# A vision-transformer block on one core: the second norm in two tile groups, expert gates by tanh, the router behind two half blocks

## The chip, the core and the metric

The kernel runs on one core of one Trainium2 chip. Its time is the device time of one execution in microseconds; before the change three executions took 165.94, 166.53 and 167.59 us (median 166.53 us). The profile is of one further execution. TensorE is called PE below, its weight loads PEld, VectorE DVE, ScalarE ACT, GpSimd POOL and SyncE SP.

## The reference

Sixteen images of 3x96x96 are cut into 36 patches each, with four shifted copies beside each channel; patches are normalised, multiplied by a 3840x192 matrix, and a class token is put in front, which gives 16 x 37 = 592 tokens of 192 numbers. One transformer layer follows:

```python
h = h + attention(layernorm(h))          # 12 heads of 16, bias by distance
h = h + ffn(layernorm(h))                # the second norm is this one

def ffn(x):                              # per token
    probs = softmax(x @ router_w)        # 8 experts
    gates, idx = top_k(probs, 2)
    gates = gates / sum(gates)
    g, u = silu(x @ w_gate[e]), x @ w_up[e]
    routed = sum of gates[e] * ((g * u) @ w_down[e])
    shared = (silu(x @ ws_gate) * (x @ ws_up)) @ ws_down     # 768 wide
    alpha = sigmoid(x @ sg_w + sg_b)
    return alpha * shared + (1 - alpha) * routed
```

Everything is float32. All eight experts are computed densely for all tokens; the gates of the ones that were not chosen are zero.

## The kernel before

**Tiles.** The 592 tokens lie in five tiles of 128 (`TILES`; the last has 80 real tokens) when tokens are on the partitions, and in two halves of 296 columns (`HALF`) when features are. Each large product is split into float16 high and low parts: a value X is kept as `XAh` (high, features 0 to 127), `XAl` (its low part), `XB` (high, features 128 to 191, twice) and `YC` (low of these). So one 128x296 product takes five matmuls, k = 0 to 4. k = 0 and 1 read `XAh`, k = 2 `XB`, k = 3 `XAl`, k = 4 `YC`.

**Stages.** Patches and tokens (to about 33 us), first norm (to 44 us), attention (to 80 us), second norm (80 to 88 us), feed-forward (from 85.85 us to the end).

**Second norm.** `wo(t)` on PE writes the attention output of tile t into PSUM, `add_attention` on DVE adds the residual, then follow statistics (`residual`, L1039), `variances` (L1049), a square root on ACT (`root`, L731), five small DVE steps (`rsqrt`, L999) and `normed` (L1060), all with one pass over five tiles for the small steps. `NORMS` (L64) lists the groups of tiles of each pass: the first norm has a group of three and a group of two, the second norm one of five. ACT duplicates 64 columns of each tile (`copies`), PE transposes (two per tile), ACT writes high parts (`high_parts`), DVE low parts (`low_parts`), each once for tiles 0 to 2 (part 0) and once for tiles 3 and 4 (part 1). `keep_warm` is a run of matmuls whose results are not used.

**Feed-forward.** There are 18 blocks f of 128 hidden columns (6 shared, 12 of experts) and two halves, so 36 half blocks i. `gu(i)` is ten matmuls (gate m = 0 and up m = 1), `silu_step(i)` on ACT, `product(i)` on DVE, `act_high(i)` on ACT and `act_low(i)` on POOL follow, and `down(f)` is fifteen matmuls for the five tiles. `gu(i)` waits for `product(i - 2)`, whose PSUM banks it takes. The PE order is gu(0) with the router in its middle, gu(1), gu(2), gu(3), then per block two `gu` and one `down` two blocks behind. A matmul needs half 0 only from tiles 0 to 2 (columns 0 to 295 of 0 to 383).

**Router and gates.** `router` (L558) is thirty matmuls of nine columns. DVE copies the logits out (L1205) and picks the two largest in chains of small dependent steps (`choose_first`, `second_largest`, `choose_second`, `gate_sum`, `gate_split`), which stand between products 0 to 4. ACT takes exponentials of logits. The gates are transposed on PE (`gates`), copied by ACT (`gate_copy`), written to DRAM and broadcast from there, to be used from block 6 on. Between its silu steps ACT also rounds the next weights (`ffn_high`), and DVE makes their low parts (`ffn_low`). The order on each engine is written out by hand; each engine runs its list in order and waits on semaphores.

Of the kernel before, what the change touches and what calls it, by code (L numbers as in the profile page):

```python
# [58 lines left out]
GATE_STEP = 6  # L59
ABUF = 3  # L60
# [3 lines left out]
NORMS = ((0, range(0, 5), 5), (10, range(0, 3), 10), (10, range(3, 5), 15), (20, range(0, 5), 20))  # L64
# [18 lines left out]
def vit_kernel(nc, x_inner, x_ring, w_inner, w_ring, gb, consts, j_rev, ind, tok_b, cls, tab,  # L83
               aw_a, aw_b, aw_c, f_a, f_b, f_d, gate_rows, out):
    with ExitStack() as ctx:
# [92 lines left out]
        def split(p):  # L178
# [28 lines left out]
                   a_first a_xh a_xsq a_s0 a_ring a_bw a_sqr a_cs a_aw a_wh a_sqrt a_hi a_k a_q a_vh a_exp a_pth a_chi a_e a_dup a_sig a_gt  # L207
                   a_fw a_silu a_ah
                   v_one v_ind v_pad v_aw0 v_jm v_jr v_xl v_fold v_wl v_awl v_mk v_stat v_h v_hn v_lo  v_vm v_xr v_sg v_max v_sub
                   v_rows v_cn v_rd v_lg v_gate v_gx v_fw v_hf v_acc v_fin v_al v_bn  # L210
# [14 lines left out]
        def wparts(c0, c1):  # L225

            return [WAh[:, c0:c1], WAl[:, c0:c1], WB[:, c0:c1], WAh[:, c0:c1], WC[:, c0:c1]]

# [66 lines left out]
        def _(pe):  # L295
# [207 lines left out]
            def wo(t):  # L503

                need = min(2 * (t + 1), PAIRS)
                pe.wait_ge(S["a_chi"], need)
                tok = slice(t * P, (t + 1) * P)
                o = PS[:, (3, 3, 4, 4, 5)[t], D * (t % 2):D * (t % 2) + D]
                mm(o, CA[:, tok], awst[:, 0, OC:OC + D], start=(t % 2 == 0), stop=False, skip_group_check=True)
                last = mm(o, CC[:, tok], awst[0:CROWS, 2, OC:OC + D], start=False, stop=True, skip_group_check=True)  # L510
                last.then_inc(S["p_wo"], 1)
# [60 lines left out]
            def gu(i):  # L572

                f, half = divmod(i, 2)
# [8 lines left out]
                for m in range(2):  # L583
                    if i == 0 and m == 1:
                        router()
                    w5 = (Ah[:, m, fc], Al[:, m, fc], Bw[:, m, fc], Ah[:, m, fc], Bw[:, m, fc])
                    for k, (w, x) in enumerate(zip(w5, yparts(cols))):
                        if i < 2 and m == 0:
                            tokens_ready(1, i, k)
                        last = mm(PS[:, 3 + 2 * (i % 2) + m, 0:HALF], w, x, start=(k == 0), stop=(k == 4))  # L590
# [44 lines left out]
        def _(act):  # L635
# [196 lines left out]
            def act_high(i):  # L832
                f, half = divmod(i, 2)
# [9 lines left out]

            for i in range(2 * FT + 1):
                if 0 <= i - 1 - GATE_STEP < 2:
                    gate_copy(i - 1 - GATE_STEP)
                if i < 2 * FT:
# [10 lines left out]
        def _(pool):  # L858
# [20 lines left out]
            def act_low(i):  # L879
                f, half = divmod(i, 2)  # L880
# [15 lines left out]
        def _(dve):  # L896
# [271 lines left out]
            def add_attention(t):  # L1168
                dve.wait_ge(S["p_wo"], (2, 2, 4, 4, 5)[t])
                return V.scalar_tensor_tensor(  # L1170
                    out=h2[:, t, :], in0=PS[:, (3, 3, 4, 4, 5)[t], D * (t % 2):D * (t % 2) + D],
# [24 lines left out]
            def over8(v):  # L1196
                return v.unsqueeze(2).to_broadcast([P, TILES, 8])

            m1, s1, m2, s2, den, rd_ = (small[:, i, :] for i in (32, 33, 34, 35, 36, 37))
# [4 lines left out]
            dve.wait_ge(S["p_r"], 1)  # L1204
            V.tensor_scalar(lg[:, :, :], PS[:, 7, 0:9 * TILES].rearrange("p (t e) -> p t e", t=TILES), 1.0 / XW, None,  # L1205
                            ALU.mult).then_inc(S["v_lg"], 1)
            dve.wait_ge(S["v_lg"], 1)
            V.tensor_reduce(m1, l8, AX.X, ALU.max).then_inc(S["v_bn"], 1)
            dve.wait_ge(S["v_bn"], bn[0] + 1)
            gstep(V.tensor_tensor(g8[:, 0], l8, over8(m1), ALU.subtract))  # L1210

            def choose_first():
                gstep(V.tensor_tensor(g8[:, 2], l8, over8(m1), ALU.is_equal))
# [4 lines left out]
            def second_largest():  # L1218
                gstep(V.scalar_tensor_tensor(out=g8[:, 5], in0=g8[:, 4], scalar=-3e38, in1=l8, op0=ALU.mult,
                                             op1=ALU.add))  # L1220
                gstep(V.tensor_reduce(m2, g8[:, 5], AX.X, ALU.max))
                gstep(V.tensor_tensor(g8[:, 6], g8[:, 5], over8(m2), ALU.is_equal))

            def choose_second():
# [3 lines left out]
                gstep(V.tensor_tensor(g8[:, 9], g8[:, 8], g8[:, 4], ALU.add))  # L1228

            def gate_sum():  # L1230
# [183 lines left out]
```

## Time and profile before

| what | value |
|---|---|
| median of three executions | 166.53 us |
| profiled execution, device time | 166.45 us |
| its span, first to last instruction | 164.6 us |
| outside the span | 1.85 us |
| PE busy | 147.1 us |
| DVE busy | 116.2 us |
| ACT busy | 89.7 us |
| POOL busy | 42.0 us |
| mean granted clock | 0.986 |

All times inside a trace count from the first instruction of the span. A timeline row gives the start, the duration, the engine, the source line, the operation and, in brackets, how long the engine was idle before it and what ended that. A row with x5 merges five instructions of one kind.

### The profile page before, as it was taken

The page shows a single profiled execution, that of the slowest core. Times are in us where ns is not written, and L with a number is a line of the kernel's source. Part 1 is how long each engine was busy: PE and PEld are TensorE (multiplying, and loading weights), DVE is VectorE, ACT ScalarE, POOL GpSimd, SP SyncE. Part 2 cuts the span into 40 slices and gives each one's busy share as a digit, 9 for nine tenths or more (in the row PEclk, how much of TensorE's full clock was granted, in tenths as well). Part 3 has the DMA queues.
Part 4 walks back from the last instruction along what each step waited for, and adds up shares of the span by engine and source line. Part 5 has one row for each costly group of instructions (what it writes and reads, how often), then busy time and mean ns, then how long its engine had stood idle before and what let it go on. Part 6 is the DMA issues. An engine that isn't in the chain of part 4 may idle for free.

```text
span 164.6 us, 4269 instructions
## 1 busy us (share of the span) xinstructions
PE 147.1 (89%) x1717; PEld 113.5 (69%) x1717; DVE 116.2 (71%) x285; ACT 89.7 (54%) x198; POOL 42.0 (26%) x55
## 2 busy tenths in 40 slices
PE   0449999999989998979998999999899999999992
PEld 0217778863658997868645677888668788788781
DVE  6299969799897678957673797785885832732753
ACT  0498797561679335453457697655465343334440
POOL 0000001000000000000000345368576677487330
PEclk9999999999999999999997899999999999999998
DMA  5999974900000000002995000258000000000003
GB/s 142 387 361 381 300 190 100 415 19 0 0 0 4 4 4 4 4 0 67 378 405 210 0 0 0 63 207 329 2 4 0 0 4 2 2 4 0 0 0 111
DMA packets 7391, 16.89 MB, mean 103 GB/s; under 512 B 800, under 2 KB 3612, under 8 KB 7372
## 3 DMA queue, kind: packets, MB, share of 16 engines
q1 hardware_dynamic: 7012, 16.29, 28.5%
q10 hardware_dynamic: 360, 0.34, 0.7%
q8 instruction: 13, 0.21, 0.6%
q14 instruction: 6, 0.05, 0.1%
HBM read 16.15 MB, written 0.47 MB: 101 GB/s over the span
## 4 chain that ended last, share of the span: by engine, by line
PE 57%; DVE 24%; ACT 7%; issue 6%; ACTq 3%; POOL 2%; DVEq 0%; POOLq 0%
PE PS L590 19%; PE PS L618 11%; PE PS L436 4%; PE PS L323 3%; PE PS L344 2%; PE PS L346 2%; PE PS L410 2%; PE PS L347 2%; DVE mx L1123 2%; DVE xsq L1127 2%; DVE hn L1064 2%; PE PS L455 2%; DVE vhl L1268 2%; PE PS L310 2%; POOL vhl L876 1%
## 5 line engine op out<-in xcount | busy, mean ns | idle before, releaser
L885 POOL TENSOR_TENSOR kq<-vhl,kq 128x296 f16<-128x296 f32 x35 | 29.4, 841 | 87.0 <-ACT kq L837 86.8
L1268 DVE SCALAR_TENSOR_TENSOR vhl<-PS,vhl 128x296 f32<-128x296 f32 x36 | 16.8, 466 | 21.9 <-POOL vhl L876 12.1
L830 ACT ACTIVATE vhl<-PS 128x296 f32<-128x296 f32 x36 | 15.0, 416 | 26.5 <-PE PS L590 26.4
L837 ACT ACTIVATE kq<-vhl 128x296 f16<-128x296 f32 x36 | 16.0, 445 | 5.4 <-DVE vhl L1268 5.4
L876 POOL TENSOR_TENSOR vhl<-vhl,xs 128x296 f32<-128x296 f32 x14 | 12.6, 900 | 5.6 <-issue 4.8
L1257 DVE TENSOR_TENSOR vhl<-vhl,xs 64x296 f32<-64x296 f32 (+1 forms) x18 | 10.2, 565 | 2.8 <-ACT vhl L830 2.6
L590 PE MATMUL PS<-XAh,piece 128*128 128x296 f16 x48 | 10.8, 310 | 0.3
L590 PE MATMUL PS<-XAh,slab 128*128 128x296 f16 x48 | 10.0, 291 | 0.9 <-DVE vhl L1268 0.9
L344 PE MATMUL PS<-whl,xhl 128*128 128x193 f16 (+1 forms) x40 | 10.6, 266 | 0.0
L346 PE MATMUL PS<-whl,xhl 128*128 128x193 f16 (+1 forms) x40 | 10.6, 265 | 0.0
L347 PE MATMUL PS<-whl,xhl 128*128 128x192 f16 (+1 forms) x40 | 10.5, 262 | 0.0
L373 PE MATMUL PS<-WAh 128*128 128x512 f16 x44 | 10.3, 380 | 0.1
L936 DVE SCALAR_TENSOR_TENSOR we<-slab,gbs,we 128x192 f32<-128x192 f32 x24 | 8.2, 414 | 3.1 <-ACT we L674 3.1
L310 PE MATMUL PS<-slab,gbs 128*32 128x192 f32 x60 | 4.5, 396 | 6.6 <-DMA slab<-in_w_inner_dram 6.6
L590 PE MATMUL PS<-XAh,xsq 128*128 128x296 f16 x48 | 10.0, 290 | 0.0
L618 PE MATMUL PS<-slab,kq 128*128 128x192 f16 x90 | 8.4, 246 | 0.3 <-DVE t L1291 0.3
L618 PE MATMUL PS<-piece,kq 128*128 128x192 f16 x90 | 8.4, 246 | 0.0
L618 PE MATMUL PS<-xsq,kq 128*128 128x192 f16 x90 | 8.2, 246 | 0.1
L618 PEld LDWEIGHTS PS<-slab,kq 128*128 128x128 f16 x90 | 7.5, 98 | 0.8 <-issue 0.6
L618 PEld LDWEIGHTS PS<-xsq,kq 128*128 128x128 f16 x90 | 7.5, 98 | 0.5 <-issue 0.3
L323 PE MATMUL PS<-xsq,one 128*32 128x296 f32 (+1 forms) x32 | 5.7, 484 | 2.4 <-ACT xsq L642 2.4
L618 PEld LDWEIGHTS PS<-piece,kq 128*128 128x128 f16 x90 | 7.6, 98 | 0.3
(215 smaller groups left out, 395.3 us busy)
## 6 DMA issues: line engine op xcount, KB each, us to landing
slab<-in_w_inner_dram SPq DMA_DIRECT2D x3, 960.0 KB, 9.5
xs<-gate_rows_dram SPq DMA_DIRECT2D x8, 296.0 KB, 5.9
xs<-in_x_inner_dram SPq DMA_DIRECT2D x3, 592.0 KB, 10.6
stage<-in_f_a_dram SPq DMA_DIRECT2D x2, 768.0 KB, 4.8
stage<-in_f_b_dram SPq DMA_DIRECT2D x2, 768.0 KB, 6.4
stage<-in_f_d_dram SPq DMA_DIRECT2D x2, 576.0 KB, 7.9
xhl<-in_f_a_dram SPq DMA_DIRECT2D x1, 768.0 KB, 8.8
xhl<-in_f_b_dram SPq DMA_DIRECT2D x1, 768.0 KB, 10.3
```

Source lines behind the costliest of these rows:

```text
L323: last = mm(PS[q:q + 32, 6 + half, 0:HALF], one[0:K, :].to_broadcast([K, 32]), xsqv[0:K, j, half * HALF:(half + 1) * HALF], start=(j < 4), ...
L344: mm(o, xh[0:K, j, tok], wh[0:K, j, :], start=(j == 0 and t % 2 == 0), stop=False, skip_group_check=True)
L346: mm(o, xl[0:K, j, tok], wh[0:K, j, :], start=False, stop=False, skip_group_check=True)
L347: last = mm(o[:, 0:D], xh[0:K, j, tok], wl[0:K, j, :], start=False, stop=(j == CHUNKS - 1), skip_group_check=True)
L373: mm(PS[:, bank, :], WAh[:, 0:P], WAh[:, 0:512], start=True, stop=True)
L590: last = mm(PS[:, 3 + 2 * (i % 2) + m, 0:HALF], w, x, start=(k == 0), stop=(k == 4))
L618: last = mm(o, a[:, f % ABUF, tok], w[:, f % PT_, :], start=(f in (0, ST) and t % 2 == 0 and k == 0), stop=(f in (ST - 1, FT - 1) and k == ...
L830: A(silu[:, i % 2, :], PS[:, 3 + 2 * (i % 2), 0:HALF], ACT.Silu, scale=1.0 / XW).then_inc(S["a_silu"], 1)
L837: A(ah[:, f % ABUF, half * HALF:(half + 1) * HALF], hf[:, i % 3, :], ACT.Copy).then_inc(S["a_ah"], 1)
L876: G.tensor_tensor(sgate[:, i % 2, :], silu[:, i % 2, :], Gb[:, f_expert(f)[0], cols], ALU.mult).then_inc(S["g_sg"], 1)
L885: G.tensor_tensor(al[:, f % ABUF, cols], hf[:, i % 3, :], ah[:, f % ABUF, cols], ALU.subtract).then_inc(S["g_al"], 1)
L1268: V.scalar_tensor_tensor(out=hf[:, i % 3, :], in0=PS[:, 4 + 2 * (i % 2), 0:HALF], scalar=SH / XW, in1=src[:, i % 2, :], op0=ALU.mult, op1= ...
```

## The change

- `NORMS`: the second norm runs in a group of tiles 0 to 2 and one of tiles 3 and 4. Tile 2's attention output moves to bank 4 alone, those of 3 and 4 to bank 5.
- DVE: variances of the first group stand before the residual of tile 3; tile 4's residual and the second group's variance stand behind the first group's `normed`; its `rsqrt` and `normed` behind the low parts of the first group; then product 0, and only then the low parts of the second group.
- The first four half blocks are now (f, half) = (0,0), (1,0), (0,1), (1,1). PE does gu(0) and gu(1), then the transposes of tiles 3 and 4, four `keep_warm` matmuls, the whole router, then gu(2). In block 0 the order of the ten matmuls is k = 0 and 1 for both m, and then k by k.
- `down(0)` and `down(1)` wait for four half blocks, where down(0) waited for two.
- ACT: a square root for the second group, a one-element silu ahead of `silu_step(0)`, then the copies and high parts of the second group. Three exponentials go; two tanh (five values per partition each) come behind `act_high(1)` and `act_high(3)`.
- Gates: with d the difference of the two largest logits, the first gate is (1 + tanh(d/2))/2 and the second (1 - tanh(d/2))/2, and alpha = (1 + tanh(l/2))/2. The chain on DVE is `choose_first` (with the copy of the logits) behind product 1, the second choice behind product 2, `gate_split` behind product 3, `gate_values` behind product 4.
- `keep_warm` in the second norm: 5 and 3 matmuls where it was 6, 4, 4 and 3.

```diff
-NORMS = ((0, range(0, 5), 5), (10, range(0, 3), 10), (10, range(3, 5), 15), (20, range(0, 5), 20))
+NORMS = ((0, range(0, 5), 5), (10, range(0, 3), 10), (10, range(3, 5), 15), (20, range(0, 3), 20),
+         (20, range(3, 5), 25))
+def half_block(i):
+    return ((0, 0), (1, 0), (0, 1), (1, 1))[i] if i < 4 else divmod(i, 2)
...
-            keep_warm(6, 6)
-            for name, count, n in (("v_h", 3 * TILES, 4), ("v_stat", 20, 4), ("v_stat", 21, 3)):
-                pe.wait_ge(S[name], count)
-                keep_warm(6, n)
-            transposes(1, (0, 1, 2), range(TILES))
+            keep_warm(6, 5)
+            pe.wait_ge(S["v_stat"], 22)
+            keep_warm(6, 3)
+            transposes(1, (0, 1, 2), range(3))
...
+                    if f == 1 and half == 0:
+                        transposes(1, (0, 1, 2), (3, 4))
+                        keep_warm(7, 4)
+                        router()
...
-                pe.wait_ge(S["a_ah"], 2 * f + 2)
-                pe.wait_ge(S["g_al"], min(2 * f + 2, 2 * FT - 1))
+                pe.wait_ge(S["a_ah"], max(2 * f + 2, 4))
+                pe.wait_ge(S["g_al"], min(max(2 * f + 2, 4), 2 * FT - 1))
...
-            copies(1, range(TILES))
+            copies(1, range(3))
             high_parts(1, (0, 1, 2), 0)
-            high_parts(1, (0, 1, 2), 1)
-            act.wait_ge(S["v_lg"], 1)
-            A(small[:, 30, :], lg[:, :, 8], ACT.Exp, scale=-1.0).then_inc(S["a_sig"], 1)
-            A(small[:, 31, :], lg[:, :, 8], ACT.Exp).then_inc(S["a_sig"], 1)
-            act.wait_ge(S["v_gate"], 1)
-            A(g8[:, 1], g8[:, 0], ACT.Exp).then_inc(S["a_e"], 1)
+            root(4)
+            A(small[:, 46, 0:1], one[:, :], ACT.Silu)
...
+            silu_step(0)
+            copies(1, (3, 4))
+            high_parts(1, (0, 1, 2), 1)
...
+                if i == 2:
+                    alpha_tanh()
+                if i == 4:
+                    gate_tanh()
...
-            residual(1, add_attention, (2, 3))
-            residual(1, add_attention, (4,))
+            residual(1, add_attention, (2,))
             variances(3)
+            residual(1, add_attention, (3,))
             rsqrt(3)
             dve.wait_ge(S["p_t"], TILES)
-            normed(1, range(TILES))
+            normed(1, range(3))
+            residual(1, add_attention, (4,))
+            variances(4)
             low_parts(1, (0, 1, 2), 0)
-            low_parts(1, (0, 1, 2), 1)
+            rsqrt(4)
+            normed(1, (3, 4))
...
-            for i in range(2 * FT):
+            product(0)
+            low_parts(1, (0, 1, 2), 1)
+            for i in range(1, 2 * FT):
                 product(i)
-                if i == 0:
+                if i == 1:
                     choose_first()
-                if i == 1:
+                if i == 2:
                     second_largest()
-                if i == 2:
                     choose_second()
                 if i == 3:
-                    gate_sum()
+                    gate_split()
                 if i == 4:
-                    gate_split()
+                    gate_values()
```

## Rows read from the trace of the kernel before

**Rows 1.** The page: busy time by engine, and PE's granted clock in 40 slices.

```profile
PE 147.1 (89%) x1717; PEld 113.5 (69%) x1717; DVE 116.2 (71%) x285; ACT 89.7 (54%) x198; POOL 42.0 (26%) x55
PEclk9999999999999999999997899999999999999998
```

**Rows 2.** Windows: length, busy time (instructions) per engine, granted clock, DMA share, GB/s.

```profile
83.93:88.30 4.37, 3.62 (x45) 2.28 (x46) 2.78 (x8) 3.85 (x10) 0.00 (x0) 0.99 1.03 408
88.30:91.79 3.49, 3.49 (x22) 2.09 (x18) 1.12 (x5) 2.25 (x5) 0.00 (x0) 0.52 0.08 31
91.80:98.67 6.87, 6.67 (x57) 4.91 (x56) 6.25 (x24) 6.14 (x14) 3.19 (x5) 1.00 0.00 0
```

**Rows 3.** Timeline of PE, from the last attention output into the feed-forward.

```profile
79.53 0.49 PE L510 MATMUL PS<-awst,we 97*128 97x192 f32 x2
...
85.85 0.41 PE L590 MATMUL PS<-XAh,piece 128*128 128x296 f16 x2
...
87.56 0.17 PE L566 MATMUL PS<-WAh,XAh 128*128 128x9 f16 x1 [0.45 <-DVE wring L1074]
...
91.81 0.42 PE L590 MATMUL PS<-XAh,piece 128*128 128x296 f16 x2
...
98.67 0.41 PE L590 MATMUL PS<-XAh,piece 128*128 128x296 f16 x2
```

**Rows 4.** Timeline of ACT, second norm and the first half blocks.

```profile
83.91 1.42 ACT L753 ACTIVATE hn<-hn 128x64 f32<-128x64 f32 x5 [1.78 <-DVE hn L1064]
85.23 0.47 ACT L746 ACTIVATE XAh<-PS 128x384 f16<-128x384 f32 x1
...
85.97 0.39 ACT L746 ACTIVATE XAh<-PS 128x256 f16<-128x256 f32 x1
...
86.65 1.28 ACT L821 ACT_TABLE_LOAD   x1
...
89.46 1.28 ACT L830 ACT_TABLE_LOAD   x1
90.75 0.42 ACT L830 ACTIVATE vhl<-PS 128x296 f32<-128x296 f32 x1
...
93.27 0.42 ACT L830 ACTIVATE vhl<-PS 128x296 f32<-128x296 f32 x1 [0.50 <-PE PS L590]
...
93.92 0.83 ACT L729 ACTIVATE slab<-stage 128x768 f16<-128x768 f32 x1
...
96.45 0.44 ACT L837 ACTIVATE kq<-vhl 128x296 f16<-128x296 f32 x1
```

**Rows 5.** Timeline of DVE in the second norm.

```profile
80.47 0.34 DVE L1170 SCALAR_TENSOR_TENSOR h<-PS,h 128x192 f32<-128x192 f32 x1
80.84 0.36 DVE L1046 BATCH_NORM_STATS2 bst<-h 128x6 f32<-128x192 f32 x1
...
82.61 0.19 DVE L1005 RECIPROCAL small<-small 128x5 f32<-128x5 f32 x1 [0.71 <-ACT small L735]
...
83.50 1.54 DVE L1064 TENSOR_SCALAR hn<-h,mv,small 128x192 f32<-128x192 f32 x5
```

**Rows 6.** The chain that ended last: start, length, line; one `down`, two `gu`.

```profile
102.25 1.24 PE PS L618 x15
103.49 2.52 PE PS L590 x20
```

**Rows 7.** Timeline of DVE, last low part, product 0 and gate steps.

```profile
87.01 0.41 DVE L1074 SCALAR_TENSOR_TENSOR wring<-PS,XB 64x256 f16<-64x256 f32 x1
88.50 0.21 DVE L1205 TENSOR_SCALAR whl<-PS 128x45 f32<-128x45 f32 x1 [1.09 <-PE PS L568]
...
91.27 0.47 DVE L1268 SCALAR_TENSOR_TENSOR vhl<-PS,vhl 128x296 f32<-128x296 f32 x1 [2.10 <-ACT vhl L830]
...
92.96 0.68 DVE L1219 SCALAR_TENSOR_TENSOR whl<-whl 128x40 f32<-128x40 f32 x1
```

**Rows 8.** Timeline of POOL: the low part of product 0.

```profile
92.85 0.74 POOL L885 TENSOR_TENSOR kq<-vhl,kq 128x296 f16<-128x296 f32 x1 [67.48 <-ACT kq L837]
```

More of the change, by code:

```diff
@@ L59 @@
 GATE_STEP = 6
+STEADY = [(k, m) for m in range(2) for k in range(5)]
+FIRST = [(0, 0), (1, 0), (0, 1), (1, 1)] + [(k, m) for k in range(2, 5) for m in range(2)]
 ABUF = 3
@@ L507, in wo @@
                 tok = slice(t * P, (t + 1) * P)
-                o = PS[:, (3, 3, 4, 4, 5)[t], D * (t % 2):D * (t % 2) + D]
-                mm(o, CA[:, tok], awst[:, 0, OC:OC + D], start=(t % 2 == 0), stop=False, skip_group_check=True)
-                last = mm(o, CC[:, tok], awst[0:CROWS, 2, OC:OC + D], start=False, stop=True, skip_group_check=True)
+                mm(attention_out(t), CA[:, tok], awst[:, 0, OC:OC + D], start=(t in (0, 2, 3)), stop=False,
+                   skip_group_check=True)
+                last = mm(attention_out(t), CC[:, tok], awst[0:CROWS, 2, OC:OC + D], start=False, stop=True,
+                          skip_group_check=True)
                 last.then_inc(S["p_wo"], 1)
@@ L572, in gu @@
             def gu(i):
-                f, half = divmod(i, 2)
+                f, half = half_block(i)
                 if i % (2 * PT_) == 0:
@@ L582, in gu @@
                 fc = slice(f % PT_ * P, (f % PT_ + 1) * P)
[L583 to L590, printed above, removed]
+                w5 = [(Ah[:, m, fc], Al[:, m, fc], Bw[:, m, fc], Ah[:, m, fc], Bw[:, m, fc]) for m in range(2)]
+                x5 = yparts(cols)
+                for k, m in FIRST if f == 0 else STEADY:
+                    if f == 0 and m == 0:
+                        tokens_ready(1, half, k)
+                    last = mm(PS[:, 3 + 2 * (i % 2) + m, 0:HALF], w5[m][k], x5[k], start=(k == 0), stop=(k == 4))
                 last.then_inc(S["p_gu"], 1)
@@ L832, in act_high @@
             def act_high(i):
-                f, half = divmod(i, 2)
+                f, half = half_block(i)
                 act.wait_ge(S["v_hf"], i + 1)
@@ L879, in act_low @@
             def act_low(i):
-                f, half = divmod(i, 2)
+                f, half = half_block(i)
                 cols = slice(half * HALF, (half + 1) * HALF)
@@ L1197, in over8 @@
                 return v.unsqueeze(2).to_broadcast([P, TILES, 8])
-            m1, s1, m2, s2, den, rd_ = (small[:, i, :] for i in (32, 33, 34, 35, 36, 37))
+            m1, s1, m2, s2, dif, both = (small[:, i, :] for i in (32, 33, 34, 35, 36, 37))
             l8 = lg[:, :, 0:8]
             rank = cst_rank[:, :].unsqueeze(1).to_broadcast([P, TILES, 8])
[L1204 to L1210, printed above, removed]
-            def choose_first():
+            def choose_first():
+                dve.wait_ge(S["p_r"], 1)
+                V.tensor_scalar(lg[:, :, :], PS[:, 7, 0:9 * TILES].rearrange("p (t e) -> p t e", t=TILES), 1.0 / XW,
+                                None, ALU.mult).then_inc(S["v_lg"], 1)
+                dve.wait_ge(S["v_lg"], 1)
+                gstep(V.tensor_reduce(m1, l8, AX.X, ALU.max))
                 gstep(V.tensor_tensor(g8[:, 2], l8, over8(m1), ALU.is_equal))
@@ L1227, in choose_second, with gate_values @@
                 gstep(V.tensor_tensor(g8[:, 8], rank, over8(s2), ALU.is_equal))
-                gstep(V.tensor_tensor(g8[:, 9], g8[:, 8], g8[:, 4], ALU.add))
-            def gate_sum():
-                dve.wait_ge(S["a_e"], 1)
-                gstep(V.tensor_tensor(g8[:, 10], g8[:, 9], g8[:, 1], ALU.mult))
-                gstep(V.tensor_reduce(den, g8[:, 10], AX.X, ALU.add))
-                gstep(V.reciprocal(rd_, den))
-            def gate_split():
-                dve.wait_ge(S["a_sig"], 2)
-                gstep(V.tensor_scalar(small[:, 40:42, :], small[:, 30:32, :], 1.0, None, ALU.add))
-                gstep(V.reciprocal(small[:, 42:44, :], small[:, 40:42, :]))
-                gstep(V.tensor_scalar(small[:, 38, :], small[:, 42, :], 1.0 / (SH * SW), None, ALU.mult))
-                gstep(V.scalar_tensor_tensor(out=small[:, 39, :], in0=rd_, scalar=1.0, in1=small[:, 43, :],
-                                             op0=ALU.mult, op1=ALU.mult))
-                V.tensor_tensor(Gf[:, :, :], g8[:, 10], over8(small[:, 39, :]), ALU.mult).then_inc(S["v_gx"], 1)
+            def gate_split():
+                dve.wait_ge(S["a_sig"], 1)
+                V.tensor_scalar(small[:, 38, :], small[:, 31, :], 0.5 / (SH * SW), 0.5 / (SH * SW), ALU.mult,
+                                ALU.add).then_inc(S["v_gate"], 1)
+                gate[0] += 1
+                gstep(V.tensor_scalar(both, small[:, 31, :], -0.25, 0.25, ALU.mult, ALU.add))
+            def gate_values():
+                dve.wait_ge(S["a_sig"], 2)
+                gstep(V.tensor_tensor(small[:, 40, :], small[:, 30, :], both, ALU.mult))
+                V.tensor_tensor(small[:, 42, :], both, small[:, 40, :], ALU.add).then_inc(S["v_gate"], 1)
+                gate[0] += 1
+                gstep(V.tensor_tensor(small[:, 43, :], both, small[:, 40, :], ALU.subtract))
+                V.tensor_tensor(g8[:, 9], g8[:, 4], over8(small[:, 42, :]), ALU.mult).then_inc(S["v_gate"], 1)
+                gate[0] += 1
+                gstep(V.tensor_tensor(g8[:, 10], g8[:, 8], over8(small[:, 43, :]), ALU.mult))
+                V.tensor_tensor(Gf[:, :, :], g8[:, 9], g8[:, 10], ALU.add).then_inc(S["v_gx"], 1)
             def product(i):
```

20 lines of the change are left out of this document (15 added, 5 removed).

## The prediction

> **What bounds the kernel now.** I read the page first: PE is busy 89% of the span, with its clock below full speed in two neighbouring slices only [rows 1]. So PE's own list sets the time wherever it does not wait. In the steady part of the feed-forward two half blocks take 2.52 us and one down product 1.24 us, with nothing between them [rows 6]; the change touches neither number. What it can win is where PE waits or runs slowly, and the windows by stage show where that is [rows 2]: from 83.93 to 88.30 PE is busy 3.62 of 4.37 us, much of it transposes, and from 88.30 to 91.79 it is nominally full but at a granted clock of 0.52.
>
> PE's timeline gives the marks [rows 3]: the last attention product ends at 79.53 + 0.49 = 80.02, gu(0) starts at 85.85, the router at 87.56, gu(2) at 91.81, gu(6), right behind down(0), at 98.67. The useful work between gu(0) and gu(6) is six half blocks (3 x 2.52), the router (87.56 to 88.30, 0.74) and a down product (1.24): 9.54 us [rows 3, 6]. It takes 98.67 - 85.85 = 12.82 us.
>
> The reasons are in ACT's timeline [rows 4]: a table load of 1.28 us for the exponentials and a second one at 89.46 for silu, so that the first silu starts at 90.75 although gu(0) was done about 89.5 (five of the fifteen matmuls that fill the 3.49 us from 88.30 [rows 2]). Product 0 runs at 91.27 for 0.47 [rows 7] and releases gu(2) at 91.81. PE's slow clock was hidden by that: gu(1) ended just as product 0 did. Since gu(2) starts when both are there, a full clock alone would have won next to nothing.
>
> **The norm in two groups.** The limit becomes the last attention product, because tile 3 shares a bank with tile 4: residual of tile 3 at 80.02 + 0.04 = 80.06, 0.34 for it, 0.36 for its statistics with 0.03 between [rows 5], so 80.8 (the 0.04 is my estimate of a hand-over). The three-tile variance and the root lie beside the wait for PE (tile 2's product is two products earlier, an estimated 1.5 us, since the last part of one alone takes 0.49 [rows 3]) and cost nothing; that cover is gone only if they take longer than this wait. From the reciprocal to normed is 83.50 - 82.61 = 0.89 [rows 5]: normed at 81.7 instead of 83.50. Normed to the first high part took 85.23 - 83.50 = 1.73 [rows 4, 5]; with three copies of 1.42/5 = 0.28 ahead of it instead of five it is no longer than that. High part to gu(0): 85.85 - 85.23 = 0.62 [rows 3, 4]. So gu(0) starts at 81.7 + 1.73 + 0.62 = 84.05, **1.8 us earlier**. Tile 4's residual, statistics and variance (0.34 + 0.36 and some 0.5 for the rest) stand on DVE between normed (ends 82.7) and the low parts, which wait for the high part until 83.9 in any case: about hidden, 0.1 us at worst, and PE has gu(0)'s first four or six matmuls meanwhile.
>
> **Block 1 ahead of the router.** gu(0) and gu(1) take 2.52 and end at 86.6. Behind ACT's two high parts (start 83.45, about 0.85) come the root (0.2), a table load of 1.28 and the one-element silu (0.2), so silu 0 starts at 86.0 and ends at 86.4. Queued behind it are the two copies (0.56). DVE has meanwhile done the low parts (to 85.0), rsqrt (0.89) and normed of two tiles (0.6), to 86.5; product 0 takes it to 86.95, beside PE's transposes. The transposes of two tiles end at 87.2. From the first high part of the small group to the end of its last low part is 87.01 + 0.41 - 85.97 = 1.45 [rows 4, 7]: 88.65. The router goes to 89.4, and gu(2) starts there, 2.4 us earlier than at 91.81. PE idles about 0.75 us before the router; the four warming matmuls lie in that wait.
>
> **Gates.** Copy of the logits and five steps of 0.21 [rows 7], with some 0.02 between them: 1.4 us from 89.6 to 91.0, just before product 2. silu(2) starts when gu(2) ends (90.65), at 90.8. On ACT silu(2) to act_high(3) was 96.45 - 93.27 = 3.18 to its start [rows 4], with a rounding of 0.83 twice in it; the tanh adds 0.2: act_high(3) at 94.2 at the earliest, 0.44 long. On DVE product 2 ends at 91.7; the eight steps of the second choice now all stand behind it, seven of them one after another, 1.6 us if all take 0.21, 2.0 us if the one beside POOL takes 0.68 again [rows 7]: 93.3 to 93.7, so product 3 ends at 93.8 to 94.15. gu(5) waits for it from 93.2: a **new wait on PE of 0.6 to 1.0 us**, where before the two chains stood behind different products. I take 1.0. gu(5) ends at 95.5. down(0) now waits for POOL's low part 3: act_high(3) ends at 94.65, POOL's 0.74 [rows 8] takes it to 95.5. Both end together. down(0) to 96.8: gu(6) starts at 96.8 instead of 98.67. gate_split and gate_values are eight steps where gate_sum and gate_split were eight; the last one ends near 96.4, before gu(6) ends at 98.05 and the transposes of the gates want it. Nothing.
>
> **From there on** every dependence is the same, so the gain is carried to the end: all weights were loaded by 88.5 (the DMA share falls to 0.08 after 88.30 [rows 2]), and the broadcast of the gates starts as much earlier as its first use. No DMA issue is moved.
>
> **The sum.** 98.67 - 96.8 = 1.9 us. Against the profiled execution, 166.45 us with 164.6 us of span and 1.85 us around it, that is 164.6 us. The median of the runs shown, 166.53, is 0.08 above it, which I neglect.
>
> **Two rules of the pages.** A load at 86.65 ends at 87.93 and the one at 89.46 is followed by silu at 90.75, within 0.01 us of its end: a switch costs 1.28 us here [rows 4]. The Trainium skill, page "ScalarE: Activation LUTs", section "What ACT_TABLE_LOAD costs", adds a drain of about 1.38 us to each, 2.66 us in all; by that, silu 0 would start about 1.4 us later than I have it and the gain would shrink to about 0.5 us. The rows speak against it.
>
> Whether tanh needs a load of its own beside silu no row shows. The same page, section "Table sets: the hidden batching unit", lists tanh in the sets of exp and of sigmoid and names no set that has silu. By that rule each tanh would bring two loads; that is the third rival.
>
> **Rivals.** (1) *The slow clock moves onto the path.* PE was granted 0.52 for 3.49 us after a stretch with transposes, waits and nine-column matmuls [rows 2]. The new order has more dense work in it (block 1, the warming matmuls), but also a wait and the router ahead of gu(2). If the low stretch covers gu(2) and gu(3), ten matmuls take 1.26/0.52 = 2.4 us; silu 2 and all behind it move by 1.15, while gu(3)'s delay is absorbed by the wait before gu(5). Gain 1.9 - 1.15 = 0.75: 165.7 us.
>
> (2) *DVE and ACT become the bound.* Before gu(6) DVE was busy 6.25 and ACT 6.14 of 6.87 us [rows 2]. They now get gu(2) to gu(5) with the same lists in a shorter time. If POOL's writes slow more of the small steps as at 92.96 (0.68 for 0.21) [rows 7], say two more, the second choice ends 1 us later and PE waits that long. Gain 0.9: 165.5 us.
>
> (3) *Slower: tanh reloads tables.* A load of 1.28 ahead of each tanh and one ahead of the silu that follows it. Silu 3 and with it product 3 move by 2.56, less the 0.4 to 0.8 us in which product 3 waits for DVE anyway; act_high(3) and down(0) move by 2.56; the second pair pushes silu 5, the later silu steps and gate_copy by 2.56 again, of which ACT's idle time there (about 1 us before silu 6) takes 1.0. In sum about 2.56 + 2.56 - 1.0 = 4.1 us: 164.6 + 4.1 = 168.7 us. It decides as soon as ACT loses more than 1.9 us in this stretch.
>
> (4) *The head start is lost before the router.* If silu 0, with the copies behind it, comes later than I have it, the transposes, the small group's parts and the router go with it one for one. It would have to be 2.4 us late to lose all of gu(2)'s head start: 166 to 166.5 us.
>
> **Chances.** My forecast (gain 1.4 to 2.5) 0.52, rival 1 0.18, rival 2 0.13, rival 3 0.06, rival 4 or something not seen 0.11, of which half slower. A measurement here can tell about 1% from no change, 1.67 us, so faster means under 164.86. The forecast's centre is only 0.26 us under that line: I give it two thirds of its 0.52 for faster, and 0.07 for a larger gain or a slower reference elsewhere, 0.42. Slower than 168.2: rival 3 and half of the unseen, 0.12. Same: 0.46. The range goes from a gain of 3.1 us (the stalls before gu(5) and down(0) gone too) to 166.7, which holds rivals 1, 2 and most of 4: 163.4 to 166.7; outside are rival 3 and the unseen on both sides.
>
> **What would show it.** One table load fewer (sqrt, silu; none at a tanh). Normed of three tiles at 81.6 to 81.8, gu(0) at 83.9 to 84.1, gu(2) at 89.3 to 89.6, gu(6) at 96.6 to 97.0, and from gu(6) to the end the same 65.9 us as before. A wait of PE before gu(5) released by a DVE product, and none before gu(2) released by one. The granted clock from 85 to 92 tells rival 1. I am wrong if normed does not start before 82.5, if an ACT table load stands next to a tanh, or if PE waits over 1.5 us before gu(5) or down(0).

## The result and the profile after

The changed kernel took 164.48 us (median of 4, 163.98 to 165.09) against 166.24 us before (median of 4); the ratio is 0.9887, 95% interval 0.9846 to 0.9929. The forecast was 164.6 us, range 163.4 to 166.7. Five further rounds later gave 164.41 us and 0.9882 (0.9853 to 0.9910). Medians in this document are over all executions of a kernel, ratios leave out those over 1.5% above its fastest. So the number was right, in part by luck. The share that the prediction gave to each cause was not, as the experiments below show.

The profiled execution took 164.49 us, with a span of 162.7 us. The page's opening lines answer to [rows 1]:

```profile
span 162.7 us, 4264 instructions
PE 143.3 (88%) x1712; PEld 111.7 (69%) x1712; DVE 117.3 (72%) x290; ACT 88.4 (54%) x198; POOL 42.2 (26%) x55
PEclk9999999999999999999999999999999999999999
```

The clock stays up in this trace. PE's timeline, with the rows that answer to [rows 3] (start, duration, engine, line, operation, idle time before it):

```profile
78.91 0.49 PE L523 MATMUL PS<-awst,we 97*128 97x192 f32 x2
...
83.33 0.66 PE L601 MATMUL PS<-XAh,piece 128*128 128x296 f16 x4 [0.67 <-ACT XAh L761]
...
88.11 0.17 PE L579 MATMUL PS<-WAh,XAh 128*128 128x9 f16 x1 [0.76 <-DVE wring L1100]
...
88.86 0.66 PE L601 MATMUL PS<-XAh,piece 128*128 128x296 f16 x4
...
93.98 0.42 PE L601 MATMUL PS<-XAh,piece 128*128 128x296 f16 x2 [1.19 <-DVE vhl L1297]
...
95.34 1.40 PE L629 MATMUL PS<-piece,kq 128*128 128x192 f16 x15
...
96.57 0.41 PE L601 MATMUL PS<-XAh,piece 128*128 128x296 f16 x2
```

These are the last attention product (end 79.40), gu(0), the router, gu(2), gu(5), down(0) and gu(6). The first mark stands 0.62 us earlier than before's 80.02. The difference is there 52 us ahead of it, in the patch stage, which the change does not touch (these rows are from the traces of before and of the changed kernel; at 14 us the two still agree within 0.2 us):

```profile
27.79 0.52 PE L310 MATMUL PS<-wring,gbs 96*32 96x192 f32 x4
27.18 0.52 PE L323 MATMUL PS<-wring,gbs 96*32 96x192 f32 x4
```

Two traces of the changed kernel differ there by as much (27.18 and 27.70), and over all traces of this study the first mark lies between 79.10 and 80.47. Marks behind it must therefore be compared as distances from it, and this is done from here on. **gu(6) starts 17.17 us after the last attention product, where it was 18.65: 1.48 us won.** From gu(6) to the end of the span it is 66.13 us, where it was 65.93. So within the trace the change wins 1.3 us, and 0.6 us of the shorter span lies in the early part. The runs say 1.8 and 2.2 us. The rest of that is not explained: the first mark is at 80.06 on average in the four traces with the old norm and order (before and tanh alone, twice each) and at 79.62 in the ten others, but the first group lies wholly within the range of the second, so whether the change also shortens the early part is not shown.

Windows by stage, to be held against [rows 2] (length, busy time and instructions of PE, PEld, DVE, ACT, POOL, then granted clock, DMA share, GB/s):

```profile
79.40:88.11 8.71, 7.10 (x44) 3.87 (x42) 6.93 (x28) 5.36 (x16) 0.21 (x1) 1.00 1.00 387
88.11:96.57 8.46, 7.27 (x85) 5.66 (x86) 6.82 (x27) 5.67 (x14) 3.07 (x5) 1.00 0.03 9
```

In both stages PE now idles more than a microsecond. ACT's timeline shows the tables, as [rows 4] did:

```profile
83.68 1.28 ACT L835 ACT_TABLE_LOAD   x1
84.97 0.20 ACT L835 ACTIVATE small<-one 128x1 f32<-128x1 f32 x1
85.08 0.40 ACT L849 ACTIVATE vhl<-PS 128x296 f32<-128x296 f32 x1
...
90.31 0.42 ACT L849 ACTIVATE vhl<-PS 128x296 f32<-128x296 f32 x1 [2.49 <-PE PS L601]
90.63 0.44 ACT L856 ACTIVATE kq<-vhl 128x296 f16<-128x296 f32 x1
90.97 0.20 ACT L839 ACTIVATE small<-whl 128x5 f32<-128x5 f32 x1
91.07 0.83 ACT L744 ACTIVATE slab<-stage 128x768 f16<-128x768 f32 x1
```

One load, for silu, then silu 0 at once; the tanh at 90.97 stands between its neighbours with no load, and ACT waits 2.49 us for PE ahead of silu 2. On DVE (normed of three tiles, the second choice, product 3) and POOL (low part 3), the rows that answer to [rows 5, 7, 8]:

```profile
81.03 0.96 DVE L1090 TENSOR_SCALAR hn<-h,mv,small 128x192 f32<-128x192 f32 x3
...
91.22 0.73 DVE L1245 SCALAR_TENSOR_TENSOR whl<-whl 128x40 f32<-128x40 f32 x1
91.98 0.20 DVE L1247 TENSOR_REDUCE small<-whl 128x5 f32<-128x40 f32 x1
...
92.98 0.44 DVE L1254 TENSOR_TENSOR whl<-cst,small 128x40 f32<-128x40 f32 x1
93.46 0.47 DVE L1297 SCALAR_TENSOR_TENSOR vhl<-PS,vhl 128x296 f32<-128x296 f32 x1
```

```profile
92.62 0.74 POOL L911 TENSOR_TENSOR kq<-vhl,kq 128x296 f16<-128x296 f32 x1 [0.73 <-ACT kq L856]
94.48 0.75 POOL L911 TENSOR_TENSOR kq<-vhl,kq 128x296 f16<-128x296 f32 x1 [1.12 <-ACT kq L856]
```

### The profile page after: what moved, and what is told of

Its sections match the earlier page's. It is cut to its first block, busy times and chain, and to the rows that moved or that the text cites. A ratio compares the mean times of both kernels' runs of the same rounds, so it can differ in the third digit from the quotient of the medians.

```text
span 162.7 us, 4264 instructions
## 1 busy us (share of the span) xinstructions
PE 143.3 (88%) x1712; PEld 111.7 (69%) x1712; DVE 117.3 (72%) x290; ACT 88.4 (54%) x198; POOL 42.2 (26%) x55
## 4 chain that ended last, share of the span: by engine, by line
PE 62%; DVE 20%; ACT 6%; issue 5%; ACTq 3%; POOL 2%; DVEq 0%; POOLq 0%
PE PS L601 22%; PE PS L629 11%; PE PS L449 4%; PE PS L336 3%; PE PS L423 2%; PE PS L359 2%; PE PS L357 2%; PE PS L360 2%; DVE mx L1149 2%; DVE xsq L1153 2%; PE PS L468 2%; PE PS L323 2%; POOL vhl L902 1%; PE PS L498 1%; DVE vhl L1297 1%
## 5 line engine op out<-in xcount | busy, mean ns | idle before, releaser
L1297 DVE SCALAR_TENSOR_TENSOR vhl<-PS,vhl 128x296 f32<-128x296 f32 x36 | 16.8, 465 | 20.3 <-POOL vhl L902 12.1
L601 PE MATMUL PS<-XAh,piece 128*128 128x296 f16 x48 | 9.6, 289 | 1.9 <-DVE vhl L1297 1.2
L357 PE MATMUL PS<-whl,xhl 128*128 128x193 f16 (+1 forms) x40 | 10.3, 257 | 0.0
L359 PE MATMUL PS<-whl,xhl 128*128 128x193 f16 (+1 forms) x40 | 10.3, 257 | 0.0
L386 PE MATMUL PS<-WAh 128*128 128x512 f16 x39 | 9.6, 380 | 0.3 <-DVE small L1033 0.2
```

What stands on the lines that cost most here:

```text
L357: mm(o, xh[0:K, j, tok], wh[0:K, j, :], start=(j == 0 and t % 2 == 0), stop=False, skip_group_check=True)
L359: mm(o, xl[0:K, j, tok], wh[0:K, j, :], start=False, stop=False, skip_group_check=True)
L601: last = mm(PS[:, 3 + 2 * (i % 2) + m, 0:HALF], w5[m][k], x5[k], start=(k == 0), stop=(k == 4))
L1297: V.scalar_tensor_tensor(out=hf[:, i % 3, :], in0=PS[:, 4 + 2 * (i % 2), 0:HALF], scalar=SH / XW, in1=src[:, i % 2, :], op0=ALU.mult, op1= ...
```

## The experiments

Each was timed beside the kernel before on its chip; ratios are to that kernel. The medians of before were 166.15, 166.35 and 166.58 us on the three chips of the experiments, so medians of two rows can differ by 0.2 to 0.4 us through the chip alone; where that matters, go by the ratios. "To gu(6)" is the distance from the end of the last attention product to the start of gu(6), read from each trace as above.

| kernel | median us | ratio, 95% interval | to gu(6) | gu(6) to end |
|---|---|---|---|---|
| before | 166.24 | 1 | 18.65 | 65.93 |
| before, second trace | 166.91, one execution | - | 18.68 | 65.96 |
| changed | 164.48 | 0.9887 (0.9846 to 0.9929) | 17.17 | 66.13 |
| changed, again | 164.41 | 0.9882 (0.9853 to 0.9910) | 17.16 | 66.11 |
| changed, five-tile norm | 166.91 | 1.0028 (0.9990 to 1.0066) | 18.98 | 66.15 |
| changed, exponentials | 165.47 | 0.9954 (0.9920 to 0.9988) | 18.28 | 65.99 |
| changed, no warming before router | 165.18 | 0.9899 (0.9827 to 0.9971) | 18.13 | 66.07 |
| changed, second choice later | 164.04 | 0.9839 (0.9781 to 0.9898) | 16.70 | 65.95 |
| before with split norm | 167.34 | 1.0067 (1.0039 to 1.0095) | 20.00 | 65.96 |
| **before with tanh** | 165.13 | 0.9911 (0.9876 to 0.9945) | 16.85 | 66.02 |
| before with tanh, again | 164.32 | 0.9863 (0.9837 to 0.9890) | 16.86 | 66.01 |
| router behind gu(2) | 162.79 | 0.9791 (0.9764 to 0.9818) | 15.50 | 66.06 |
| and down(0) waits for three | 163.02 | 0.9773 (0.9741 to 0.9806) | 14.66 | 66.37 |
| and gates one half block later | 161.60 | 0.9723 (0.9683 to 0.9763) | 14.66 | 65.67 |

The last column moves by less than 0.25 us except where two waits are taken away at the end, so the second-last column holds nearly the whole story.

### Five-tile norm in the changed kernel

```diff
-NORMS = (..., (20, range(0, 3), 20), (20, range(3, 5), 25))
+NORMS = (..., (20, range(0, 5), 20))
...
-            variances(3)
-            residual(1, add_attention, (3,))
+            residual(1, add_attention, (3, 4))
+            variances(3)
             rsqrt(3)
-            normed(1, range(3))
...
+            normed(1, range(TILES))
```

> The changed kernel with its second norm in one group of five tiles again (small steps, variance and root once for all five; the warming matmuls of the old norm); block 1 ahead of the router, the tanh gates and all else stay. Theory A (the gain is the head start of the three-tile group, and block 1 only fills the wait for the small group): normed starts about 1.7 us later after the last attention product, gu(2) and gu(6) about 1.2 to 1.7 us later than in the changed kernel, time about 1.5 us above it (166.0). Rival B (the gain is the order behind the norm): time within 0.5 us of the changed kernel (164.5).

PE's rows, last attention product, gu(0), gu(6):

```profile
78.68 0.49 PE L522 MATMUL PS<-awst,we 97*128 97x192 f32 x2
...
84.95 0.66 PE L601 MATMUL PS<-XAh,piece 128*128 128x296 f16 x4 [0.67 <-ACT XAh L761]
...
98.15 0.41 PE L601 MATMUL PS<-XAh,piece 128*128 128x296 f16 x2
```

gu(0) at +5.78 instead of +3.93, gu(6) at +18.98 instead of +17.17: in this order the whole 1.8 us of the split norm's head start is carried on. Theory A holds, with more than its 1.5 us: the order without the split is no faster than the kernel before (ratio 1.0028).

### Exponentials in the changed kernel

```diff
+            def gate_exps():
+                act.wait_ge(S["v_lg"], 1)
+                A(small[:, 30, :], lg[:, :, 8], ACT.Exp, scale=-1.0).then_inc(S["a_sig"], 1)
+                A(small[:, 31, :], lg[:, :, 8], ACT.Exp).then_inc(S["a_sig"], 1)
+                act.wait_ge(S["v_gate"], 2)
+                A(g8[:, 1], g8[:, 0], ACT.Exp).then_inc(S["a_e"], 1)
...
-                if i == 2:
-                    alpha_tanh()
-                if i == 4:
-                    gate_tanh()
+                if i == 1:
+                    gate_exps()
```

> The changed kernel with the three exponentials, the sum and the reciprocals of the old gates instead of the two tanh, the exponentials between act_high(0) and silu_step(2), where the logits are first there. Theory A: ACT is idle for 2.49 us before silu 2 in the changed kernel, so the load for exp hides and the load back to silu does not: silu 2 at about 91.2 instead of 90.3, time 0.7 to 1.2 us above the changed kernel. Rival B (DVE's second choice bounds gu(5) in any case): under 0.3 us above it.

ACT's rows, the two loads and silu 2:

```profile
88.07 1.28 ACT L839 ACT_TABLE_LOAD   x1
...
90.22 1.28 ACT L848 ACT_TABLE_LOAD   x1
91.52 0.42 ACT L848 ACTIVATE vhl<-PS 128x296 f32<-128x296 f32 x1
```

The first load hides in ACT's wait, the second does not. gu(6) moves by 1.11 us, the median by 1.0 (ratio 0.9954 against 0.9887). Theory A holds.

### The second choice one product later

```diff
                 if i == 2:
                     second_largest()
-                    choose_second()
                 if i == 3:
+                    choose_second()
                     gate_split()
```

> The changed kernel with choose_second (three dependent steps) moved from behind product 2 to behind product 3, before gate_split. Theory A (the 1.36 us wait of PE before gu(5) is DVE's chain of steps between product 2 and product 3): that wait falls to 0.5 us or less; down(0) then waits for POOL's low part 3 instead, which is about 0.6 us earlier than now; time 0.4 to 0.7 us below the changed kernel. Rival B (the wait only moves whole to down(0), through ACT's list): no change within 0.2 us.

PE's rows for gu(5), down(0) and gu(6):

```profile
93.09 0.43 PE L601 MATMUL PS<-XAh,piece 128*128 128x296 f16 x2 [0.25 <-DVE vhl L1297]
...
94.91 1.40 PE L629 MATMUL PS<-piece,kq 128*128 128x192 f16 x15 [0.39 <-issue]
96.15 0.41 PE L601 MATMUL PS<-XAh,piece 128*128 128x296 f16 x2
```

The idle time ahead of gu(5) falls from 1.19 to 0.25 us, and 0.39 us appear ahead of down(0). gu(6) is at +16.70, 0.47 us earlier, and the median 0.4 us lower, though its interval overlaps the changed kernel's. As theory A had it, DVE's chain made the wait; of the 0.94 us that left it, about half only moved.

### No warming matmuls before the router

```diff
                         transposes(1, (0, 1, 2), (3, 4))
-                        keep_warm(7, 4)
                         router()
```

> The changed kernel without the four warming matmuls between the transposes of tiles 3 and 4 and the router. Theory A (they keep the clock up): the granted clock falls to half for some 3.4 us from about 88 to 92 and gu(2), gu(3) run at half speed; time 0.7 to 1.2 us above the changed kernel. Rival B (block 1 is dense enough to keep it): clock stays 1.00, no change within 0.2 us.

Windows of this kernel, columns as above:

```profile
86.00:88.00 2.00, 0.38 (x10) 0.22 (x9) 1.09 (x3) 1.30 (x4) 0.40 (x1) 1.00 0.83 334
88.00:90.00 2.00, 2.00 (x36) 1.53 (x34) 1.12 (x7) 0.00 (x0) 0.35 (x1) 0.76 0.06 15
90.00:92.00 2.00, 2.00 (x9) 1.18 (x8) 0.81 (x3) 1.22 (x4) 0.39 (x1) 0.50 0.00 0
92.00:94.00 2.00, 2.00 (x15) 1.37 (x13) 1.79 (x8) 1.42 (x4) 0.58 (x2) 0.88 0.00 0
```

PE was busy 0.38 us in 86 to 88, and then the granted clock fell to the lower of its levels, 1.2 GHz, over gu(2) and gu(3). It cost 0.96 us to gu(6). In the three other runs the mean clock was 0.998 to 1.00 and they still took 164.36, 165.33 and 165.25 us. So the trace supports theory A, but four runs cannot say how often the clock falls, nor why the others were not at 164.5.

### The kernel before with its norm split

```diff
+            residual(1, add_attention, (2,))
+            variances(3)
+            residual(1, add_attention, (3,))
...
+            normed(1, range(3))
+            residual(1, add_attention, (4,))
+            variances(4)
             low_parts(1, (0, 1, 2), 0)
+            rsqrt(4)
+            normed(1, (3, 4))
...
                     if i == 0 and m == 1:
+                        transposes(1, (0, 1, 2), (3, 4))
+                        keep_warm(7, 4)
                         router()
```

> The kernel before with only its second norm in two groups (and bank 5 for tiles 3 and 4, and the transposes of tiles 3 and 4 and four warming matmuls ahead of the router, which still stands in the middle of gu(0)); exponentials and block order as before. Theory A (the small group is later than in a norm of five tiles, so that a split needs block 1 ahead of the router): gu(0) starts 1.8 us earlier after the last attention product but the router 0.5 to 1.0 us later, and silu 0 with it; time 0.4 to 1.0 us above the kernel before. Rival B (the early start of the norm is the gain by itself): 1.0 us or more below it.

PE's rows, last attention product, gu(0), router, gu(6):

```profile
78.75 0.49 PE L516 MATMUL PS<-awst,we 97*128 97x192 f32 x2
...
83.18 0.41 PE L597 MATMUL PS<-XAh,piece 128*128 128x296 f16 x2 [0.67 <-ACT XAh L753]
...
88.03 0.17 PE L571 MATMUL PS<-WAh,XAh 128*128 128x9 f16 x1
...
99.24 0.41 PE L597 MATMUL PS<-XAh,piece 128*128 128x296 f16 x2
```

gu(0) comes 1.89 us earlier (+3.94), but the router at +8.79 where it was 87.56 - 80.02 = 7.54: 1.25 us later (0.5 to 1.0 was expected), and the exponentials and silu 0 behind it. gu(6) is 1.35 us later, the median 1.0. In this trace the granted clock was 0.50 from 86 to 88, under the four warming matmuls. That did not set the router back: it starts 0.15 us behind the end of DVE's last low part (87.88), just as in the changed kernel at full clock (87.96 and 88.11). Theory A holds: splitting the norm makes its second group later, and a kernel that needs all tiles soon loses by it.

### The kernel before with tanh alone

```diff
-            A(small[:, 30, :], lg[:, :, 8], ACT.Exp, scale=-1.0).then_inc(S["a_sig"], 1)
-            A(small[:, 31, :], lg[:, :, 8], ACT.Exp).then_inc(S["a_sig"], 1)
-            act.wait_ge(S["v_gate"], 1)
-            A(g8[:, 1], g8[:, 0], ACT.Exp).then_inc(S["a_e"], 1)
...
+                if i == 2:
+                    alpha_tanh()
+                if i == 4:
+                    gate_tanh()
```

DVE computes the gates by the formulas of the changed kernel, but its steps stand where they stood before, the second choice spread over products 1 and 2.

> The kernel before with only its gates by tanh (no exponentials, so no table load for exp and the silu table loaded right behind the high parts); norm, block order and router as before. Theory A (the two table loads and the slow clock held gu(2) together): silu 0 starts right behind gu(0), near 89.3. With a full clock gu(2) starts at 90.2 to 90.4 instead of 91.8 and the time is 1.0 to 1.5 us below the kernel before; in a run whose clock falls from 88.3 to 91.8, gu(1) still ends at 91.8 and nothing is won. Rival B (the loads were hidden behind PE anyway): no change in either.

> The kernel before with only its gates by tanh, again, beside the changed kernel. Theory A: equal within 0.3 us. Rival B: 0.5 us or more above the changed kernel.

> The changed kernel once more, on one chip with the next one. Theory A (the gain of the change is that of its tanh; split norm and block order win only what they cost): within 0.3 us of the kernel before with tanh alone. Rival B (each part adds its own gain, 0.7 us for split and order, 1.2 us for tanh): 0.5 us or more below it.

ACT's rows of the first of these kernels, load and silu 0:

```profile
86.74 1.28 ACT L833 ACT_TABLE_LOAD   x1
89.23 0.42 ACT L833 ACTIVATE vhl<-PS 128x296 f32<-128x296 f32 x1 [1.21 <-PE PS L590]
```

and PE's, last attention product, gu(2) and gu(6):

```profile
79.64 0.49 PE L510 MATMUL PS<-awst,we 97*128 97x192 f32 x2
...
90.29 0.41 PE L590 MATMUL PS<-XAh,piece 128*128 128x296 f16 x2
...
96.98 0.41 PE L590 MATMUL PS<-XAh,piece 128*128 128x296 f16 x2
```

The load for silu now lies under the router, and silu 0 starts at +9.10 instead of 90.75 - 80.02 = 10.73. **gu(6) is at +16.85: 1.80 us won by tanh alone, 0.3 us more than by the whole change.** Side by side on one chip in five rounds the two take 164.32 and 164.41 us, with ratios of 0.9863 and 0.9882. Within these intervals they are equal. Rival B, that each part adds its own gain, falls.

Where do split and order go? gu(2) is at +10.16 here and at +9.46 in the changed kernel, so they do bring gu(2) 0.70 us forward. From gu(2) to gu(6) the changed kernel then takes 7.71 us and this one 6.69: it loses the lead, and 0.3 us more, mostly in the wait before gu(5): 1.19 us idle there, while here PE idles 0.21 us ahead of gu(4) and not at all ahead of gu(5).

The expectation also said that nothing is won in an execution whose clock falls. Two of the twelve executions had a mean granted clock of 0.987; they took 166.62 and 166.94 us, as long as the kernel before. The ten of the changed kernel all had 0.996 or more. No trace of such an execution was taken, and two in twelve against none in ten does not show that the whole change protects the clock. Nor was it tried to keep the exponentials in the old order, but behind silu 0.

### The kernel before, a second trace

> The kernel before once more, for a second trace of it. The trace shown of before has a clock of 0.986. Theory A (my prediction: a full clock alone wins next to nothing): with the clock at 1.00 gu(2) to the end takes the same time, gu(2) starts when product 0 ends, and gu(6) starts 18.5 to 18.7 us after the last attention product, as in the trace shown. Rival B (the slow clock cost the following half blocks too): 0.4 us or more less than that.

Windows of this trace:

```profile
88.00:90.00 2.00, 2.00 (x41) 1.72 (x42) 0.60 (x3) 1.02 (x5) 0.00 (x0) 1.00 0.57 223
90.00:92.00 2.00, 0.79 (x7) 0.39 (x4) 0.31 (x1) 1.89 (x3) 0.00 (x0) 1.00 0.00 0
```

At full clock PE is through with gu(1) early and idles, busy 0.79 of 2 us, until silu 0 and product 0 are there; gu(6) is at +18.68, as with the slow clock (+18.65). Theory A holds. One thing speaks against it: on each of the three chips the executions of before with a mean clock of 0.986 (seven in all, 166.7 to 167.8 us) were slower than those at 1.00 there (medians 165.99, 166.35 and 166.55 us), by 0.6 to 0.8 us in the median. Their low stretch may have lain elsewhere; no trace of one was taken, and this stays open.

### Router behind gu(2), then two waits less

```diff
                     if f == 1 and half == 0:
                         transposes(1, (0, 1, 2), (3, 4))
-                        keep_warm(7, 4)
+                        keep_warm(7, 3)
+                    if f == 1 and half == 1:
                         router()
...
-                if i == 2:
+                if i == 3:
                     alpha_tanh()
...
-                if i == 1:
+                if i == 2:
                     choose_first()
-                if i == 2:
+                if i == 3:
                     second_largest()
-                    choose_second()
-                if i == 3:
-                    gate_split()
                 if i == 4:
+                    choose_second()
+                    gate_split()
+                if i == 5:
                     gate_values()
```

> The changed kernel with the router behind gu(2) instead of ahead of it, three warming matmuls instead of four, the tanh of alpha one half block later, and each part of the gate chain on DVE one product later (choose_first behind product 2, second_largest behind 3, choose_second and gate_split behind 4, gate_values behind 5). Theory A (PE idles 0.76 us ahead of the router although the high parts that gu(2) begins with are there, and DVE's chain holds gu(5)): gu(2) starts 1.4 us earlier, the wait before gu(5) is gone, gu(6) starts 1.5 to 2.0 us earlier than in the changed kernel; time 162.5 to 163.3. Rival B (the chain on DVE is as long and the wait goes to gu(4) or to the transposes of the gates): 0.5 us or less is won.

PE's gu(2), router, down(0), gu(6), and POOL's low part 3:

```profile
87.89 0.66 PE L601 MATMUL PS<-XAh,piece 128*128 128x296 f16 x4
89.14 0.17 PE L579 MATMUL PS<-WAh,XAh 128*128 128x9 f16 x1
...
94.50 1.40 PE L629 MATMUL PS<-piece,kq 128*128 128x192 f16 x15 [0.67 <-issue]
95.74 0.41 PE L601 MATMUL PS<-XAh,piece 128*128 128x296 f16 x2
```

```profile
93.66 0.74 POOL L912 TENSOR_TENSOR kq<-vhl,kq 128x296 f16<-128x296 f32 x1 [0.73 <-ACT kq L857]
```

With the last attention product ending at 80.24 in this trace, gu(2) is at +7.65 and gu(6) at +15.50, 1.67 us better than in the changed kernel and 1.35 better than with tanh alone; the median is 162.79 us. Theory A holds. What is left is a wait ahead of down(0) until POOL's low part of half block 3 (it ends at 94.40). But down(0) reads block 0, half blocks 0 and 2. The next edits take that away, and then move the gates:

```diff
-                pe.wait_ge(S["a_ah"], max(2 * f + 2, 4))
-                pe.wait_ge(S["g_al"], min(max(2 * f + 2, 4), 2 * FT - 1))
+                pe.wait_ge(S["a_ah"], max(2 * f + 2, 3))
+                pe.wait_ge(S["g_al"], min(max(2 * f + 2, 3), 2 * FT - 1))
```

> The kernel with the router behind gu(2), where down(0) and down(1) wait for three half blocks on ACT and POOL (down(1) is behind the fourth in any case through its own product) instead of four: down(0) reads block 0 alone, half blocks 0 and 2. Theory A (PE waits 0.85 us ahead of down(0) for POOL's low part 3, which it does not need): down(0) starts behind gu(5), but the gates' transposes then wait for gate_values, which ends at about 96.75: half of it is won, time 0.3 to 0.8 us below the kernel with the router behind gu(2). Rival B (the gates' last step takes it all): no change.

```diff
-GATE_STEP = 6
+GATE_STEP = 7
```

> The same, with the transposes of the gates, their copies and so the broadcast one half block later on PE and ACT. Theory A: no wait for gate_values is left and the whole 0.85 us is won, 161.8 to 162.2 us. Rival B (the broadcast, whose first use is some 1.2 us behind its landing, becomes late for block 6): a wait of PE in block 6 or 7 takes back what is won or more.

PE's down(0), gu(6) and the gates' transposes with the first of the two edits:

```profile
93.90 1.40 PE L629 MATMUL PS<-piece,kq 128*128 128x192 f16 x15
95.13 0.41 PE L601 MATMUL PS<-XAh,piece 128*128 128x296 f16 x2
...
97.04 0.60 PE L611 MATMUL PS<-cst,whl 128*8 128x128 f32 x4 [0.49 <-DVE whl L1274]
```

gu(6) is 0.84 us earlier, and PE then idles 0.49 us for DVE's last gate step (the rest of gu(6) to end grows by 0.3). In the runs the first edit shows no gain of its own, where 0.3 to 0.8 us was expected: 163.02 against 162.79 us, not timed side by side, with overlapping intervals. With the gates later as well the wait is gone and the broadcast is not late (behind gu(6) PE's waits are those of before, without the one for the gates): 161.60 us, the fastest version of the study, 2.8% below before (0.9683 to 0.9763). On the same chip tanh alone took 164.32 us, so with the router moved and these two waits gone, split and order do pay. What the same two edits would win with the old norm was not tried.

## Why the prediction was right, and where it was not

- **The stages up to gu(2)** came as worked out, as distances from the last attention product: normed at +1.63 (forecast 1.7), gu(0) +3.93 (4.0), gu(2) +9.46 (9.4). The hand-over of 0.04 us from PE to DVE, which no row showed, measured 0.11 (the product ends at 79.40, tile 3's residual starts at 79.51). The variance and root hidden beside the wait for PE, and tile 4's residual beside the high part, cost nothing.
- **The wait before gu(5)** was there, released by product 3, and larger: gu(4)'s last matmul starts at 92.50 and gu(5) at 93.98, some 1.36 us lost behind the 0.12 of a matmul, where I took 1.0. Half of the excess is that product 2 ended at +11.90 where I had +11.68. The rest is the chain: I counted eight steps, seven of them dependent, where the kernel has seven and six; two of these began while POOL was writing and took 0.73 and 0.44 us instead of 0.20, and I had priced one such step. From the end of product 2 to the end of product 3 it took 2.63 us, not 2.45. That wait is the term that was mis-sized. gu(6) is at +17.17, not +16.8.
- **down(0)** started at 95.34, when gu(5)'s matmuls were through (95.25) and POOL's low part 3 had just ended (95.23): both together, as forecast. That this wait covers one half block more than it needs, I did not see.
- **The tables**: a tanh needs no load beside silu, so the third rival falls; silu 0 follows its load without a drain, as before. The loads at 83.68 here and at 90.22 in the kernel with exponentials start within 0.02 us of the end of the instruction before them, and the next one starts within 0.02 us of their own end. On both the trace decides against what I had derived from the Trainium skill's page "ScalarE: Activation LUTs": for tanh from section "Table sets: the hidden batching unit", for the drain from section "What ACT_TABLE_LOAD costs".
- **The clock**: it did not fall in the trace of the changed kernel, and the trace without the warming matmuls shows what the first rival would have cost, 0.96 us (I had 1.15). That a full clock by itself wins nothing in this stage held in the second trace of before; the times of its other executions leave a doubt.
- **What failed is the credit.** I read that the two table loads held gu(2), and then let the gain begin with "the norm in two groups", whose head start of 1.8 us I carried through to the sum, with the tanh as a condition. Never did I price tanh by itself. Alone it wins as much as the whole change: without exponentials silu 0 starts right behind gu(0), and the old five-tile norm with the old order reaches gu(6) sooner (+16.85) than the changed kernel. The split alone costs 1.35 us to gu(6), the order with the five-tile norm 0.33 us even with tanh, both together without tanh win 0.37 us. The gains do not add: what split and order are worth hangs on the tables and on what stands behind them. Of the split's head start of 1.8 us, 1.1 is used up by the router, which comes later after the last attention product than before (+8.71, before +7.54), so that gu(2) leads tanh alone by 0.70 only, and the gate chain takes that and 0.3 more.
- **The span of 162.7 us** is the forecast's to the tenth, but by two errors that cancel: the stage won 1.3 us instead of 1.9, and the early part of that execution was 0.6 us shorter, of which the model said nothing. That is luck.

## What to carry to other kernels

Price each part of a compound change alone, also the one that looks like a mere substitution: here replacing exponentials by a function that needs no table load of its own gave the whole gain by itself, and the other parts paid only after further edits. A stage that is split to start earlier can end later, as here; it pays only if what is moved ahead fills the gap until the second part, and if what waits for all parts (here the router) is moved behind something that does not. When a wait goes, look at what the next wait really needs: a count that is one too high held gu(6) back by 0.84 us in the trace here, though the time fell only when the next wait, for the gates, went too.

## What the runs showed of the hardware

- Two small DVE steps (40 values per partition, 0.20 us as a rule) took 0.73 and 0.44 us in the changed kernel: they began while POOL ran an operation of 0.75 us on SBUF (91.15 and 92.62) and ended 0.05 us behind it (91.95 and 93.42). So did a step of only five values that started at 94.54 and took 0.72. All three read two inputs from SBUF; a reduction beside POOL (92.76), which reads one, took its 0.20. Such chains are longer than their steps add up to. Whether it is the number of inputs that decides was not tried.
- The time from the start of the span to the last attention product scattered between 79.10 and 80.47 us over traces of kernels whose code is the same up to there or nearly so. A difference of spans under 1.4 us between two single traces says little here; distances between marks agreed within 0.03 us between repeated traces.
